# A two-stage expert kernel: the two choices of a token told apart by expert number, and the lower rows of five sequences gathered during the last choice tiles

## The chip, the cores and the metric

The kernel runs on one core of a Trainium2 chip. The metric is the time of one execution in device microseconds (us), the median of several runs. Engines work side by side: TensorE (PE, with its weight loads PEld), VectorE (DVE), ScalarE (ACT), GpSimd (POOL) and SyncE (SP), which here only issues DMAs. An engine takes its instructions in the order of its program and is held by waits on semaphores.

## The reference, cut to what matters

The input x has 16 sequences of 256 tokens with 256 features. A first block (attention, and eight experts with one choice for each token) adds to x. The second block is what the change touches. Every token chooses two of eight experts; a shared expert is added; the result goes, sequence by sequence, through two of eight gated experts.

```python
scores = softmax(logits)                     # a token's eight experts
topk_w, topk_idx = top_k(scores, 2)          # its two choices
topk_w = topk_w / (topk_w.sum(-1) + 1e-20)
y_all = einsum('etm,emh->eth', leaky(x @ w_gate) * (x @ w_up), w_down)
y = (y_all[topk_idx, token] * topk_w).sum(1) + p      # p: shared expert
...
logits = y.mean(axis=1) @ gate_w.T + gate_b  # per sequence
gates = softmax(two highest logits)
out = x + sum over the two e of gates[e] * gelu(y @ expert_w[e].T + expert_b[e])
```

The sum over a token's two choices has the same value in either order.

## The kernel before, in words

The choices of all tokens (2*4096) are sorted by expert into tiles of 128 rows; each expert begins a tile of its own, so there are TILES2 = 71 tiles at most. `pos_k_i[:, c, k]` is the place of choice k of the tokens of chunk c in the sorted order, `w_k` the choice's weight, `tstart2` the first tile of each expert.

The **choice stage** works tile by tile. POOL gathers the 128 input rows of a tile (`choice_rows`, an indirect DMA at L917, three buffers `c_gath`). TensorE transposes them (L1583), multiplies by the tile's expert (L1591), transposes the product three tiles later (`choice_turn`, L1599) and multiplies by the down weights (L1605). VectorE forms the product (L2860, L2862, tile i-1 in pass i of its loop) and copies the transposed product of tile i-3 out of PSUM (L2856); `choice_turn` of the next tile waits for that copy (`c_mtc`). ScalarE copies the result (`c_y`, three buffers), and SP stores it to `y2_dram` (L807), each store counted on one of three semaphores `c_st`.

The **gated stage** works on the 16 sequences b in order. When all stores of the choice stage have landed, POOL gathers for each sequence four times 128 rows of `y2_dram`: two chunks (n) of tokens by two choices (k). The buffers `yk` are three deep, so the gathers of sequence b wait for the sum of b-3 (`d_z`). Behind each gather is a memset on POOL (`space`, L947) on which POOL waits. VectorE's `sum_choices` (L2883, four instructions: k = 0 for both chunks, then k = 1) adds the weighted rows to the shared expert's result `p_s`. TensorE transposes the sum (`turn_z`, L1642), ScalarE copies it with its mean, TensorE multiplies for the gate logits (L1656), VectorE takes the two highest, and TensorE multiplies by the chosen experts (bias L1663, weights L1669). In one step TensorE does `turn_z(b)`, the rest of sequence b-1 and the first half expert of b; in the step of the last sequence one product of sequence 14 is ahead of `turn_z(15)`. VectorE's order in a step is: last addition of b-2, gates of b, first addition of b-1, sum of b+1. The first sums lie among the last shared experts.

At the start SP issues the loads of the first block; its last one is w1 (8 MB, L721). The next DMA in its queue is the store of the late rows `h_late` (L725), for which it waits on `hnorm`. This is the branch that the profiled run takes (`Else`).

Of the kernel before, what the change touches and what calls it, by code (L numbers as in the profile page):

```python
# [3 lines left out]
def bass_adaln_ffn_kernel(  # L4
# [18 lines left out]
    P = 128  # L23
# [31 lines left out]
    RT = 3  # L55
# [4 lines left out]
    with ctx:  # L60
# [300 lines left out]
        yk = [N.take(2 * NB, D) for _ in range(RT)]  # L361
        z_s = [N.take(NB, D) for _ in range(RT)]
        z_t = [N.take(KD, S) for _ in range(RT)]
# [44 lines left out]
        tile_f2 = Q.take(TILES2)  # L408

        NLB = NU // 4  # L410
        lgt_2 = Q.take(S)
        wt_g = router_g
# [122 lines left out]
        d_pos = sem("d_pos")  # L535
# [18 lines left out]
        d_got = [sem(f"d_got{k}") for k in range(3)]  # L554
# [13 lines left out]
        last_got = c_got[0:2]  # L568
        last_got0 = [16 * len(range(u, TILES2, RT)) for u in range(2)]
# [69 lines left out]
        def _(sp):  # L639
# [42 lines left out]

            general = branch(sp)

            with sp.If(general):
# [14 lines left out]

                sp.wait_ge(o_ps, B)
# [6 lines left out]
            with sp.Else():  # L708
# [12 lines left out]
                sp.dma_start(big_w[:, :], w1).then_inc(ld_w1, 16)  # L721

# [80 lines left out]
            for n in range(NEB):  # L803
                sp.dma_start(eb_rows[n:n + 1, :].rearrange("a (p k) -> a p k", k=EBW), eb_part[n]).then_inc(eb_set, 16)
            for i in range(TILES2):
                sp.wait_ge(c_yc, i + 1)
                sp.dma_start(y2_dram[i * P:(i + 1) * P, :], c_y[i % RT]).then_inc(c_st[i % RT], 16)  # L807
# [19 lines left out]
        def _(pool):  # L827
# [159 lines left out]

            for u in range(RT):
                pool.wait_ge(c_st[u], 16 * len(range(u, TILES2, RT)))

            def rows_again(b):
                hold(pool, d_e, 2 * B + E2 * b)
                pool.tensor_copy(pos_b[:, :, :], pos_k_i[:, bass.ds(b * NB, NB), :]).then_inc(d_pos, 1)
                hold(pool, d_pos, b + 1)
                for n in range(NB):
                    for k in range(2):
                        gather_rows(yk[0][:, 2 * n + k, :], y2_dram, pos_b[:, n, k:k + 1], d_back)

            for b in range(B):
                if b >= RT:  # L1000
                    pool.wait_ge(d_z, b - RT + 1)
                parts = ([(n, k, d_got[b % RT]) for n in range(NB) for k in range(2)] if b < B - 1 else
                         [(0, 0, last_got[0]), (1, 0, last_got[0]), (0, 1, last_got[1]), (1, 1, d_got[b % RT])])
                for n, k, done in parts:
                    gather_rows(yk[b % RT][:, 2 * n + k, :], y2_dram, pos_k_i[:, b * NB + n, k:k + 1], done)
                    space()
# [1844 lines left out]

# [218 lines left out]
```

## Time and profile before

| | us |
|---|---|
| median of 3 runs | 588.18 |
| lowest and highest | 587.75, 590.46 |
| the profiled execution | 589.62 |
| its span, first to last instruction | 587.9 |

| engine | busy us | share |
|---|---|---|
| PE | 558.1 | 95% |
| PEld | 463.4 | 79% |
| DVE | 321.1 | 55% |
| ACT | 243.1 | 41% |
| POOL | 233.9 | 40% |

The next four lines divide the span in 40 slices of 14.7 us. A digit is the busy share in tenths.

```profile
PE   7999999988999999999999989999999998998886
DVE  3877758676322225733538754444444344666665
POOL 2312211042111121007546365555555078777860
DMA  5960000186995522513395035565655322444441
```

The choice stage runs from about 340 to 468 us, the gated stage's gathers from 471 to 570 us. TensorE is busy in nearly all slices; its lowest shares are in the first slice and in the last four. POOL has a slice of 0 just ahead of the gated stage's gathers and then its highest shares. The DMA engines are idle in the slices from 44 to 103 us.

### The profile page before, as it was taken

How to read it: one execution, taken by the hardware profiler on the slowest of the kernel's cores; microseconds unless marked ns; L12 is line 12 of the kernel's file. 1: busy time of each engine (PE TensorE's matmuls, PEld its weight loads, DVE VectorE, ACT ScalarE, POOL GpSimd, SP SyncE). 2: the span in 40 equal slices, each digit the busy share in tenths (PEclk: the TensorE clock that was granted, in tenths of full speed). 3: DMA queues.
4: the chain of work that ended last, by engine and by line, in shares of the span. 5: the costliest groups of instructions: out<-in, count | busy, mean ns of one | idle time of the engine just before them, and what ended most of it. 6: DMA issues, size and time to landing. Idle time of an engine off the chain costs nothing.

```text
span 587.9 us, 11468 instructions
## 1 busy us (share of the span) xinstructions
PE 558.1 (95%) x3816; PEld 463.4 (79%) x3816; DVE 321.1 (55%) x967; ACT 243.1 (41%) x670; POOL 233.9 (40%) x319
## 2 busy tenths in 40 slices
PE   7999999988999999999999989999999998998886
PEld 4788887744999999988888968888878887776664
DVE  3877758676322225733538754444444344666665
ACT  1555444660211111116544245555555454443432
POOL 2312211042111121007546365555555078777860
PEclk9999999999999999999999999999999999999999
DMA  5960000186995522513395035565655322444441
GB/s 149 387 284 4 1 1 2 64 366 254 325 345 191 184 68 73 153 64 74 76 308 191 0 100 148 160 159 150 161 153 153 96 78 85 136 129 121 127 134 56
DMA packets 48853, 83.96 MB, mean 143 GB/s; under 512 B 8946, under 2 KB 41587, under 8 KB 47252
## 3 DMA queue, kind: packets, MB, share of 16 engines
q1 hardware_dynamic: 40676, 60.97, 29.7%
q0 software_dynamic: 8112, 22.16, 15.5%
q8 instruction: 36, 0.59, 0.4%
q14 instruction: 29, 0.24, 0.1%
HBM read 62.25 MB, written 20.84 MB: 141 GB/s over the span
## 4 chain that ended last, share of the span: by engine, by line
PE 70%; POOL 12%; DVE 5%; issue 5%; DMA 4%; ACT 2%; another core or an unknown queue 0%; SPq 0%; POOLq 0%; DVEq 0%; ACTq 0%
POOL arena L917 10%; PE psum L1331 10%; PE psum L1344 9%; PE psum L1591 9%; PE psum L1503 7%; PE psum L1605 5%; PE psum L1187 5%; PE psum L1159 5%; PE psum L1520 3%; PE psum L1583 3%; DMA arena<-x,row_tok 3%; POOL iota_i L947 2%; PE psum L1167 2%; PE psum L1538 1%; PE psum L1181 1%
## 5 line engine op out<-in xcount | busy, mean ns | idle before, releaser
L917 POOL DMA_INDIRECT arena<-x,row_tok x71 | 68.1, 959 | 55.7 <-PE psum L1583 47.2
L917 POOL DMA_INDIRECT arena<-y_sorted,pos_k_i x64 | 65.3, 1021 | 35.2 <-issue 16.1
L1591 PE MATMUL psum<-big_w,arena 128*128 x284 | 72.9, 379 | 0.0
L1927 ACT ACTIVATE arena<-psum,arena 128x128 f32<-128x128 f32 x64 | 18.2, 368 | 106.5 <-PE psum L1331 85.0
L1669 PE MATMUL psum<-big_w,arena 128*128 x248 | 61.3, 379 | 0.0
L1331 PEld LDWEIGHTS psum<-arena,big_w 128*128 128x128 f32 x512 | 59.5, 192 | 1.7 <-issue 1.0
L1331 PE MATMUL psum<-arena,big_w 128*128 128x128 f32 x512 | 59.8, 275 | 0.8 <-DVE arena L2624 0.8
L1503 PE MATMUL psum<-arena,big_w 128*128 128x256 f32 x256 | 59.9, 381 | 0.2 <-ACT arena L1946 0.2
L1591 PEld LDWEIGHTS psum<-big_w,arena 128*128 128x128 f32 x284 | 53.7, 190 | 7.2
L1344 PE MATMUL psum<-arena 128*128 128x256 f32 (+1 forms) x256 | 57.7, 379 | 0.0
L2860 DVE SCALAR_TENSOR_TENSOR arena<-arena 128x128 f32<-128x128 f32 x71 | 20.8, 293 | 62.2 <-ACT arena L2013 62.2
L1503 PEld LDWEIGHTS psum<-arena,big_w 128*128 128x128 f32 x256 | 47.3, 190 | 7.1 <-ACT arena L1946 0.9
L1344 PEld LDWEIGHTS psum<-arena 128*128 128x128 f32 x256 | 47.5, 190 | 5.8
L1669 PEld LDWEIGHTS psum<-big_w,arena 128*128 128x128 f32 x248 | 45.7, 190 | 6.7
L917 POOL DMA_INDIRECT arena<-h_late,row_tok x16 | 15.3, 959 | 81.7 <-PE psum L1319 69.6
L1605 PE MATMUL psum<-big_w,arena 128*128 x142 | 44.1, 392 | 1.3 <-ACT arena L2010 1.3
L892 POOL TENSOR_TENSOR arena<-arena 128x512 f32<-128x512 f32 x16 | 19.0, 1191 | 59.9 <-DVE arena L2223 59.8
L2010 ACT COPY arena<-psum 128x256 f32<-128x256 f32 x71 | 26.4, 372 | 22.2 <-PE psum L1605 19.5
L1187 PE MATMUL psum<-arena 128*128 128x256 f32 x144 | 32.7, 380 | 0.4 <-ACT arena L1806 0.4
L1159 PE MATMUL psum<-arena 128*128 128x128 f32 x256 | 32.6, 289 | 0.0
L1520 PE MATMUL psum<-big_w,arena 128*128 128x256 f32 x128 | 30.6, 382 | 1.3 <-ACT arena L1950 1.3
L1159 PEld LDWEIGHTS psum<-arena 128*128 128x128 f32 x256 | 31.4, 204 | 0.3 <-DVE arena L2223 0.2
(338 smaller groups left out, 997.8 us busy)
## 6 DMA issues: line engine op xcount, KB each, us to landing
y_sorted<-arena SPq DMA_DIRECT2D x71, 128.0 KB
big_w<-w SPq DMA_DIRECT2D x8, 1024.0 KB, 5.3
tokens<-x SPq DMA_DIRECT2D x4, 1024.0 KB, 13.3
x<-tokens SPq DMA_DIRECT2D x16, 256.0 KB, 2.6
out<-arena SPq DMA_DIRECT2D x15, 256.0 KB
y_late<-arena SPq DMA_DIRECT2D x16, 128.0 KB, 1.7
big_w<-expert_w_t SPq DMA_DIRECT2D x1, 2048.0 KB, 7.4
arena<-x,row_tok POOLq DMA_INDIRECT x71
```

What stands on the lines that cost most here:

```text
L917: pool.indirect_dma_start(dst, None, rows, bass.IndirectOffsetOnAxis(ap=idx, axis=0)).then_inc(done, 16)
L1159: mm = pe.matmul(bank[a][:, (j % 4) * P:(j % 4 + 1) * P], wq_s[:, k, j * P:(j + 1) * P], xt_l[:, k, :], start=k == 0, stop=k == KD - 1)
L1187: mm = pe.matmul(bank[6][:, 0:D], lhs(j), wo_s[:, j, :], start=j == 0, stop=j == NPAIR - 1)
L1331: mm = pe.matmul(bank[1 + 2 * u + f // 4][:, (f % 4) * P:(f % 4 + 1) * P], big_w[:, c:c + P], g_t[u][:, k, :], start=k == 0, stop=k == KD - 1)
L1344: mm = pe.matmul(bank[5 + j % 2][:, 0:D], act_t[j % 2][:, f, :], arena[:, bass.ds(e * (NF * D) + f * D, D)], start=f == 0, stop=f == NF - 1)
L1503: mm = pe.matmul(bank[up_bank(b) + q][:, half * S:(half + 1) * S], w[:, k, q * M1:(q + 1) * M1], p_s[:, unit(b)[1][k], :], start=k == 0, s ...
L1520: mm = pe.matmul(bank[6][:, n * D:(n + 1) * D], mid[u][q][:, n * P:(n + 1) * P], md_s[:, E1 + q, :], start=q == 0, stop=q == NSH - 1)
L1591: mm = pe.matmul(bank[2 + i % RT][:, 0:2 * M1], c_gt[i % RT][:, k, :], mgu_s[:, k, bass.ds(e, 1), :].rearrange("p a m -> p (a m)"), start= ...
L1605: pe.matmul(bank[5][:, 0:D], c_midt[i % RT], md_s[:, bass.ds(e, 1), :].rearrange("p a d -> p (a d)"), start=True, stop=True).then_inc(c_dn, 1)
L1669: mm = pe.matmul(o, z_t[u][:, k, n * P:(n + 1) * P], ew_s[:, k, bass.ds(e, 1), :].rearrange("p a d -> p (a d)"), start=False, stop=n == NB ...
L2010: act.copy(c_y[t % RT], bank[5][:, 0:D]).then_inc(c_yc, 1)
L2860: dve.scalar_tensor_tensor(c_mid[v], c_leak[v], 0.01, c_leak[v], ALU.mult, ALU.max).then_inc(c_lkd, 1)
```

## The change

The places of a token's two choices are put in order on VectorE: `pos_k_i[:, :, 0]` becomes the lower place (the expert with the lower number), `pos_k_i[:, :, 1]` the upper one, and the weights `w_k` are exchanged with them. Lower rows never lie in tiles of the last expert, so they are complete when the tiles ahead of `tstart2[7]` are stored; the number of stores on each `c_st` is worked out and read into registers on POOL. The lower rows get five buffers `y_lo` outside the memory of the choice stage, the upper ones three buffers `y_hi` in it. The lower rows of sequences 0 to 4 are gathered when POOL has issued its gathers of input rows and that number of stores is reached. Then, with all stores landed, come the upper rows of 0, 1 and 2, and from sequence 3 on: wait for the sum of b-3, upper rows of b, lower rows of b+2. So that no row of `y2_dram` is read that was never written, SP copies x over it early, in three DMAs from DRAM to DRAM (9088 rows of 1 KB), and waits for them ahead of the first store. TensorE's program is the same.

```diff
@@ memory @@
-        yk = [N.take(2 * NB, D) for _ in range(RT)]
+        y_hi = [N.take(NB, D) for _ in range(RT)]
         z_s = [N.take(NB, D) for _ in range(RT)]
+        assert N.at <= NC * D + RT * (2 * D + KD * P + 3 * M1)
+        N.at = NC * D + RT * (2 * D + KD * P + 3 * M1)
+        NLO = 5
+        y_lo = [N.take(NB, D) for _ in range(NLO)]
...
+        NFILL = -(-TILES2 * P // T)
@@ SP @@
+            def fill_choice():
+                for r0 in range(0, TILES2 * P, T):
+                    n = min(T, TILES2 * P - r0)
+                    sp.dma_start(y2_dram[r0:r0 + n, :], x[0:n, :]).then_inc(filled, 16)
...
                 sp.dma_start(wo_s, wo.rearrange("(j p) n -> p j n", p=P)).then_inc(ld_wo, 16)
                 sp.dma_start(big_w[:, :], w1).then_inc(ld_w1, 16)
+                fill_choice()
...
+            sp.wait_ge(filled, 16 * NFILL)
             for i in range(TILES2):
                 sp.wait_ge(c_yc, i + 1)
@@ POOL @@
             for i in range(TILES2):
                 choice_rows(i)
 
+            def low_rows(b):
+                for n in range(NB):
+                    gather_rows(y_lo[b % NLO][:, n, :], y2_dram, pos_k_i[:, b * NB + n, 0:1], d_lo[b % NLO])
+                    space()
+
+            def high_rows(b):
+                for n in range(NB):
+                    gather_rows(y_hi[b % RT][:, n, :], y2_dram, pos_k_i[:, b * NB + n, 1:2], d_hi[b % RT])
+                    space()
+
+            pool.wait_ge(table, 4)
+            for u in range(RT):
+                hold(pool, c_st[u], pool.value_load(stores_i[0:1, u:u + 1], min_val=16, max_val=16 * len(range(u, TILES2, RT))))
+            for b in range(NLO):
+                low_rows(b)
             for u in range(RT):
                 pool.wait_ge(c_st[u], 16 * len(range(u, TILES2, RT)))
+            for b in range(RT):
+                high_rows(b)
+            for b in range(RT, B):
+                pool.wait_ge(d_z, b - RT + 1)
+                high_rows(b)
+                if b + NLO - RT < B:
+                    low_rows(b + NLO - RT)
...
-            for b in range(B):
-                if b >= RT:
-                    pool.wait_ge(d_z, b - RT + 1)
-                parts = ([(n, k, d_got[b % RT]) for n in range(NB) for k in range(2)] if b < B - 1 else
-                         [(0, 0, last_got[0]), (1, 0, last_got[0]), (0, 1, last_got[1]), (1, 1, d_got[b % RT])])
-                for n, k, done in parts:
-                    gather_rows(yk[b % RT][:, 2 * n + k, :], y2_dram, pos_k_i[:, b * NB + n, k:k + 1], done)
-                    space()
@@ VectorE @@
+            def by_expert():
+
+                for u in range(RT):
+                    g = dve.tensor_scalar(first_i[:, u:u + 1], tstart2[:, E1 - 1:E1], float(RT - 1 - u), 21846.0, ALU.add, ALU.mult)
+                link(dve.tensor_tensor(lower, pos_k[:, :, 0], pos_k[:, :, 1], ALU.is_lt))
+                link(dve.tensor_scalar(first_i, first_i, 16, None, ALU.logical_shift_right))
+                dve.tensor_copy(first_f, first_i)
+                link(dve.tensor_scalar(higher, lower, -1.0, 1.0, ALU.mult, ALU.add))
+                dve.tensor_scalar(stores_i[:, :], first_f, 1.0, 16.0, ALU.max, ALU.mult)
+                dve.tensor_tensor(pos_k_i[:, :, 0], pos_k[:, :, 0], pos_k[:, :, 1], ALU.min)
+                link(dve.tensor_tensor(pos_k_i[:, :, 1], pos_k[:, :, 0], pos_k[:, :, 1], ALU.max))
+                dve.sem_inc(table, 1)
+                dve.tensor_tensor(w_lo, w_k[:, :, :], lower.unsqueeze(1).broadcast_to([P, 2, NC]), ALU.mult)
+                link(dve.tensor_tensor(w_hi, w_k[:, :, :], higher.unsqueeze(1).broadcast_to([P, 2, NC]), ALU.mult))
+                dve.tensor_tensor(w_k[:, 0, :], w_lo[:, 0, :], w_hi[:, 1, :], ALU.add)
+                dve.tensor_tensor(w_k[:, 1, :], w_lo[:, 1, :], w_hi[:, 0, :], ALU.add)
+
+            SORT_AT = 12
             for i in range(TILES2 + LAG):
                 if i >= LAG:
...
                     dve.tensor_tensor(c_mid[v], c_mid[v], bank[2 + v][:, M1:2 * M1], ALU.mult).then_inc(c_md, 1)
+                if i == SORT_AT:
+                    by_expert()
...
-                split = isinstance(b, int) and b == B - 1
-                if split:
-                    dve.wait_ge(last_got[0], last_got0[0] + 32)
-                else:
-                    hold(dve, d_got[u], 64 * turn_no + 64)
+                dve.wait_ge(d_lo[b % NLO], 32 * (b // NLO) + 32)
...
                 for k in range(2):
                     if k:
+                        dve.wait_ge(d_hi[u], d_hi0[u] + 32 * turn_no + 32)
                         hold(dve, d_z1, b + 1)
                     for n in range(NB):
-                        if split and k:
-                            dve.wait_ge((last_got[1], d_got[u])[n], (last_got0[1], 64 * turn_no)[n] + 16)
...
-                        m = dve.scalar_tensor_tensor(z_s[u][:, n, :], yk[u][:, 2 * n + k, :], w_k[:, k, bass.ds(b * NB + n, 1)], base,
+                        m = dve.scalar_tensor_tensor(z_s[u][:, n, :], (y_hi[u] if k else y_lo[b % NLO])[:, n, :], w_k[:, k, bass.ds(b * NB + n, 1)], base,
                                                      ALU.mult, ALU.add)
```

`link` adds a wait on VectorE's own semaphore behind an instruction.

## Rows read from the trace of the kernel before

**Rows 1.** Chain of waits of the last 148 us, shares by line

```profile
by line: POOL arena L917 40.3%; issue 15.7%; POOL iota_i L947 8.8%; PE psum L1591 6.4%; PE psum L1605 4.5%; PE psum L1669 4.2%; DMA arena<-x,row_tok 3.2%; DMA arena<-y_sorted,pos_k_i 1.8%; PE psum L1503 1.8%; PE psum L1583 1.7%; DMA y_sorte
```

**Rows 2.** Timeline (start us, us, engine line op tiles [idle before]), TensorE, turn_z

```profile
499.91 0.66 PE L1642 MATMUL psum<-ident,arena 128*128 128x128 f32 x4 [0.76 <-DVE arena L2883]
...
531.75 0.66 PE L1642 MATMUL psum<-ident,arena 128*128 128x128 f32 x4
...
568.37 0.66 PE L1642 MATMUL psum<-ident,arena 128*128 128x128 f32 x4 [0.64 <-DVE arena L2883]
...
575.01 0.60 PE L1642 MATMUL psum<-ident,arena 128*128 128x128 f32 x4
```

**Rows 3.** Timeline, VectorE, sums of sequences 0, 2 and 14

```profile
478.91 1.79 DVE L2883 SCALAR_TENSOR_TENSOR arena<-arena,w_k 128x256 f32<-128x256 f32 x4
...
498.06 1.79 DVE L2883 SCALAR_TENSOR_TENSOR arena<-arena,w_k 128x256 f32<-128x256 f32 x4
...
566.52 1.80 DVE L2883 SCALAR_TENSOR_TENSOR arena<-arena,w_k 128x256 f32<-128x256 f32 x4 [0.49 <-issue]
```

**Rows 4.** Timeline, POOL, gathers of input rows and of results

```profile
454.93 0.94 POOL L917 DMA_INDIRECT arena<-x,row_tok  x1 [0.73 <-PE psum L1583]
...
470.87 0.94 POOL L917 DMA_INDIRECT arena<-y_sorted,pos_k_i  x1 [15.00 <-DMA y_sorted<-arena]
...
472.31 0.95 POOL L917 DMA_INDIRECT arena<-y_sorted,pos_k_i  x1 [0.27 <-POOL iota_i L947]
...
501.17 0.95 POOL L917 DMA_INDIRECT arena<-y_sorted,pos_k_i  x1 [0.27 <-POOL iota_i L947]
...
533.80 0.95 POOL L917 DMA_INDIRECT arena<-y_sorted,pos_k_i  x1 [0.27 <-issue]
...
541.18 0.95 POOL L917 DMA_INDIRECT arena<-y_sorted,pos_k_i  x1 [0.27 <-issue]
...
563.37 0.95 POOL L917 DMA_INDIRECT arena<-y_sorted,pos_k_i  x1 [0.27 <-issue]
```

**Rows 5.** Busy time by stretch (PE, PEld, DVE, ACT, POOL, clock, DMA share, GB/s)

```profile
350.00:400.00 50.00, 48.29 (x261) 40.75 (x259) 22.73 (x88) 28.56 (x89) 27.72 (x30) 1.00 0.57 153
```

**Rows 6.** Timeline, VectorE, small instructions of both routings

```profile
136.59 0.17 DVE L2577 TENSOR_TENSOR arena<-arena 128x8 f32<-128x8 f32 x1
136.67 0.16 DVE L2578 TENSOR_TENSOR arena<-arena 128x8 f32<-128x8 f32 x1
136.87 0.17 DVE L2579 SCALAR_TENSOR_TENSOR arena<-arena 128x8 f32<-128x8 f32 x1
...
315.53 0.65 DVE L2805 TENSOR_SCALAR arena<-pos_k_i 128x64 int32<-128x64 int32 x1
...
316.21 0.20 DVE L2806 CAST arena<-arena 128x64 f16<-128x64 int32 x1
```

**Rows 7.** Timeline, copy and next transpose's weight load at the change's tile

```profile
364.03 0.28 DVE L2856 COPY arena<-psum 128x128 f32<-128x128 f32 x1
...
364.75 0.14 PEld L1599 LDWEIGHTS psum<-ident,arena 128*128 128x128 f32 x1
```

**Rows 8.** Timeline, TensorE, gate logits of 14 and last bias product

```profile
570.45 0.61 PE L1656 MATMUL psum<-big_w,arena 128*128 128x8 f32 x4 [0.55 <-ACT arena L2019]
...
578.58 0.39 PE L1663 MATMUL psum<-big_w,ones_bf 128*128 x1 [0.46 <-issue]
```

**Rows 9.** Timeline, SP's issues of w1 and of h_late

```profile
13.59 1.44 SPq L721 DMA_DIRECT2D big_w<-w  x1
...
111.23 0.29 SPq L725 DMA_DIRECT2D h_late<-arena  x1
```

**Rows 10.** DMA issues, 0 to 150 us: w1 (count, us from issue to landing)

```profile
big_w<-w SPq DMA_DIRECT2D x1, 28.0
```

**Rows 11.** Busy time by stretch, columns as in rows 5

```profile
10.00:20.00 10.00, 9.13 (x109) 8.52 (x108) 5.00 (x10) 2.84 (x6) 4.67 (x10) 1.00 0.96 217
...
40.00:50.00 10.00, 10.00 (x133) 8.55 (x131) 8.15 (x15) 5.74 (x12) 2.39 (x2) 1.00 0.01 2
```

More of the change, by code:

```diff
@@ L408, in bass_adaln_ffn_kernel @@
         tile_f2 = Q.take(TILES2)
+        first_i = Q.take(RT).bitcast(I32)
+        first_f = Q.take(RT)
+        stores_i = sb("stores_i", [P, RT], I32)
+        lower = Q.take(NC)
+        higher = Q.take(NC)
+        w_lo = Q.take(2, NC)
+        w_hi = Q.take(2, NC)
         NLB = NU // 4
         lgt_2 = Q.take(S)
+        assert N.at <= E0 * NF * D + Q.at
         wt_g = router_g
@@ L534, in bass_adaln_ffn_kernel @@
         d_back = sem("d_back")
-        d_pos = sem("d_pos")
         d_log = sem("d_log")
@@ L553, in bass_adaln_ffn_kernel @@
         c_st = [sem(f"c_st{k}") for k in range(3)]
-        d_got = [sem(f"d_got{k}") for k in range(3)]
+        d_lo = [sem(f"d_lo{k}") for k in range(NLO)]
+        filled = sem("filled")
         d_st = [sem(f"d_st{k}") for k in range(3)]
@@ L567, in bass_adaln_ffn_kernel @@
         half_st0 = 16 * len(range(0, TILES2, RT))
-        last_got = c_got[0:2]
-        last_got0 = [16 * len(range(u, TILES2, RT)) for u in range(2)]
+        d_hi, d_hi0 = c_got, [16 * len(range(u, TILES2, RT)) for u in range(RT)]
+        NFILL = -(-TILES2 * P // T)
         l_rows_ev, l_beat_g, ld_rest = ld_x[2], ld_x[1], ld_x[3]
@@ L721, in _ @@
                 sp.dma_start(big_w[:, :], w1).then_inc(ld_w1, 16)
+                fill_choice()
                 late_rows = h_late[1:, :].rearrange("(c p) d -> p c d", p=P)
@@ L986, in _ @@
                 choice_rows(i)
+            def low_rows(b):
[11 more added lines that the diff above has]
+                low_rows(b)
             for u in range(RT):
                 pool.wait_ge(c_st[u], 16 * len(range(u, TILES2, RT)))
+            for b in range(RT):
[5 more added lines that the diff above has]
+                    low_rows(b + NLO - RT)
             def rows_again(b):
                 hold(pool, d_e, 2 * B + E2 * b)
-                pool.tensor_copy(pos_b[:, :, :], pos_k_i[:, bass.ds(b * NB, NB), :]).then_inc(d_pos, 1)
-                hold(pool, d_pos, b + 1)
+                pool.tensor_copy(pos_b[:, :, :], pos_k_i[:, bass.ds(b * NB, NB), :]).then_inc(paced, 1)
+                hold(pool, paced, spaced[0] + b + 1)
                 for n in range(NB):
-                    for k in range(2):
-                        gather_rows(yk[0][:, 2 * n + k, :], y2_dram, pos_b[:, n, k:k + 1], d_back)
-            for b in range(B):
-                if b >= RT:
-                    pool.wait_ge(d_z, b - RT + 1)
-                parts = ([(n, k, d_got[b % RT]) for n in range(NB) for k in range(2)] if b < B - 1 else
-                         [(0, 0, last_got[0]), (1, 0, last_got[0]), (0, 1, last_got[1]), (1, 1, d_got[b % RT])])
-                for n, k, done in parts:
-                    gather_rows(yk[b % RT][:, 2 * n + k, :], y2_dram, pos_k_i[:, b * NB + n, k:k + 1], done)
-                    space()
+                    gather_rows(y_lo[0][:, n, :], y2_dram, pos_b[:, n, 0:1], d_back)
+                    gather_rows(y_hi[0][:, n, :], y2_dram, pos_b[:, n, 1:2], d_back)
             with pool.If(more_gates(pool)):
@@ L2992, in every_expert @@
                         base = z_s[0][:, n, :] if k else p_s[:, bass.ds(b * NB + n, 1), :].rearrange("p a d -> p (a d)")
-                        m = dve.scalar_tensor_tensor(z_s[0][:, n, :], yk[0][:, 2 * n + k, :], w_k[:, k, bass.ds(b * NB + n, 1)], base,
+                        m = dve.scalar_tensor_tensor(z_s[0][:, n, :], (y_hi if k else y_lo)[0][:, n, :], w_k[:, k, bass.ds(b * NB + n, 1)], base,
                                                      ALU.mult, ALU.add)
```

## The prediction, made before the changed kernel was run

> **What bounds the kernel now.** The change touches only the work from the choice tiles to the end, and I read that part from its end backwards. In the chain of waits over the last 148 us [rows 1], 40.3% is the GpSimd gather line L917 and 8.8% the memset L947 that spaces the gathers, against 4.2% for the gated experts' matmuls L1669. That share is no measure of the gain: it is counted along the one chain that ended last, and other limits stand close behind. The starts of a sequence's transposes (turn_z, L1642) show where gathers decide [rows 2]. From sequence 2 at 499.91 to sequence 8 at 531.75 a step takes 31.84/6 = 5.31 us, and sequence 8 starts with no idle time on PE. The next six steps, to sequence 14 at 568.37, take 36.62 us, 6.1 each, and at the end of them PE idles 0.64 us on VectorE's weighted sum L2883. That sum itself had to wait [rows 3]: sequence 14's starts at 566.52, after 0.49 us idle, and its last gather [rows 4] starts at 563.37, so it takes 0.95 to run and 2.2 more to land. Gathers thus bound only sequences 9 to 14. Before these the loop of transposes, copy, gate logits, gates on VectorE and next sum does, at 5.31 us.
>
> POOL stood idle 15.00 us before the first of these gathers [rows 4]: its last gather of input rows starts at 454.93, and then it waits for the last store of the choice tiles. In the stage of those tiles TensorE has no slack: 48.29 of 50 us busy [rows 5].
>
> **What the change does, part by part.** *The sort block at tile 12 costs time.* It puts 14 VectorE instructions (by_expert) behind product 11 and ahead of the copy L2856 that TensorE's next transpose needs. Five are followed by a wait on VectorE's own semaphore, nine are not. Small ones of this kind [rows 6] start 0.20 us after a waited one (136.87 after 136.67) and 0.08 after another (136.67 after 136.59): 5*0.20+9*0.08 = 1.7 us at 8 columns. Six here have 32 columns and two 64, where a cast lasts 0.20 instead of 0.17, so I take 2.0. A 64-column shift of integers lasts 0.65 [rows 6]; two or three at that price make 3.0, the upper bound. At that tile [rows 7] the copy runs from 364.03 to 364.31, and the weight load of the transpose that needs it starts at 364.75: a cover of 0.44. Nothing gives the rest back later, since TensorE is busy through every tile. Stall: 2.0-0.44 = **1.6 us lost**, between 1.3 and 2.6, and all that follows moves by it.
>
> *Ten gathers move into the idle 15 us.* The lower rows of sequences 0 to 4 need only tiles of experts 0 to 6. By the reference's routing of the drawn inputs expert 7 begins at tile 58 of 71, so the stores waited for come some ten tiles before the last, and have landed when POOL has issued its last input gather (454.93+0.94+1.6 = 457.5). Three register loads come first. No row shows one on POOL; the nearest is TensorE before a product that needs loaded numbers, 0.46 us idle for two [rows 8]. I take 1.1 for the three with their waits, bounds 0.5 and 3. Ten gathers at the pitch of 1.44 (472.31 after 470.87 [rows 4]) then end at 458.6+14.4 = 473.0, after the last store has landed (470.2+1.6 = 471.8). The two upper rows of sequence 0 have landed 2.9+2.2 us later, at 478.1; the sum takes them in its second half, at 478.91+1.6+0.9 = 481.4 [rows 3]. This first sum was not late before either, so the move gains nothing here; only the lead may count later. Beside the last tiles one gather per 1.44 us takes the place of one per tile (1.6 us), nearly the same load on the DMA engines, and I cost it at nothing, 0 to 0.5.
>
> *What the gain can be.* With no gather late, the six steps after 531.75 take 31.8 us instead of 36.6: 4.8. The step from 14 to 15 (6.64 us [rows 2]) has an order of its own; in it PE idles 0.55 us for ScalarE's copy, at the gate logits [rows 8], which may go too or come back. After 575.01 nothing waits for a gather. So 4.8 to 5.3 us, middle **5.05**.
>
> *What POOL gives back.* Ten gathers of lead are not kept. The upper rows of sequence b wait for sum b-3, and queued behind that wait are the lower rows of b+2, which sum b+2 needs. The early sums come when TensorE's order lets them, not when gathers land: sum 2 ends at 498.06+1.79+1.6 = 501.45 [rows 3], and only there may the upper rows of sequence 5 start. In the kernel before sequence 5 starts at 501.17 [rows 4]. Counted from there, the last upper row of 14 is gather 38 (the lower rows of 15 lie ahead of it), where it was gather 40: two fewer, not ten. It is also needed 0.9 us later, in the sum's second half. By the old stream it starts at 563.37-3.0+0.3 = 560.7 and lands at 563.8. It is needed at 564.2: turn of 14 at 531.75+31.8+1.6 = 565.2, less 1.9 from the sum's start to the turn (568.37-566.52), plus 0.9. In time by 0.4. But the old stream was quick in its second part, where VectorE was held back: 15 pitches of 1.48 from 541.18 to 563.37, against 20 of 1.63 from 501.17 to 533.80 at full pace; the four between took 7.4, 0.9 more than at 1.63 [rows 4]. All at 1.63, and with those 0.9 again, gather 38 starts at 501.45+37*1.63+0.9 = 562.7, lands at 565.8, **1.6 late**. Between 0 and 1.6 I take **0.8**, since a stream that is late slows VectorE and so comes back toward 1.48. Sequence 15's upper rows follow 2.9 us later before a step of 6.1: not late.
>
> The GPSIMD Engine Reference of the Trainium skill (Specifications) says that GpSimd shares its SBUF interface with VectorE and contends with its two-port modes and its instructions with two SBUF inputs. The sums have two such inputs, and the pitches of 1.63 and 1.48 agree with it. By that rule a VectorE that waits less makes the gathers slower, which is rival B below.
>
> *The copy of x into the sorted rows.* SP gets three more DMAs, 9.3 MB from DRAM to DRAM, queued behind w1 and ahead of the h_late stores [rows 9]. w1 is issued at 13.59 and lands 28.0 us later [rows 10], the stores come at 111.23, and from 40 us on the DMA engines are idle (share 0.01 [rows 11]). That leaves 111.2-41.6 = 69.6 us, so the copy is hidden from 134 GB/s up. No row shows a transfer from DRAM to DRAM; the nearest low rate of a busy stretch is 217 GB/s (10 to 20 us [rows 11]), at which it takes 43 us. Cost: nothing, and no gain, as nothing waits for it. The wait on "filled", ahead of the first store of choice rows after 345 us, is long satisfied.
>
> DMA: Bandwidth & Descriptors of the Trainium skill (Where 436 GB/s comes from) gives about 358 GB/s of HBM for a core. By that the copy takes 52 us, an estimate that counts its reads and its writes, and the sum stays the same.
>
> *Edits with one answer.* A sum has one more wait, satisfied while it waits for its own first half; the last sequence's split waits go; TensorE's order stays.
>
> **The sum.** On the profiled execution (589.62 us, of which 587.9 is the span; 1.4 above the median of 588.18): +1.6-5.05+0.8 = -2.65. On the median: **585.5 us**.
>
> **The rivals.** *A, the gathers are never late again.* For it: gather 38 in time by 0.4 at the old pitches. Against it: the pitch of 1.63. It gives 588.2+1.6-5.3 = 584.5, and 584.2 with the smallest stall.
> *B, gathers bound again, at 1.63.* For it: VectorE runs at full pace nearly all the way. It gives 588.2+1.6-5.05+1.6 = 586.4, and 587.7 with the dear sort block and the small gain.
> *C, the early gathers aren't early,* because POOL's register loads and waits take as long as the last stores. For it only that no row shows such a wait on POOL. All 64 gathers then follow the last store: 588.2+1.6 = 589.8, within what is called no change.
> *D, slower: the copy of x is still running when h_late must be stored.* It decides below 134 GB/s. At 100 it ends at 41.6+93 = 134.6 and moves all that follows by 23 us: 611. Against it: the rate of 217, and 70 us of gap.
>
> **How the numbers follow.** Chances: my forecast 0.35 (its own range 584.8 to 586.4), A 0.30, B 0.17, C 0.07, D 0.06, others 0.05. The bounds of the terms reach from 588.2+1.3-5.3 = 584.2 to 588.2+2.6-4.8+1.6 = 587.6; with the scatter of a median of such runs I give 583.8 to 587.9, which leaves out C and D. A measurement of this kernel can tell about 0.5%, 2.9 us, so faster means below 585.24. That is A and a third of my forecast, 0.42; the rest of it with B and C is 0.50; slower is D and a part of the others, 0.08.
>
> **What the profile after would show.** Right: 14 small VectorE instructions near 364 that take 2.0 us, and TensorE idle 1.6 us behind them; ten gathers from about 458.6 to 473; POOL idle before sequences 4 and 5; the turn of sequence 8 near 533.3, steps of 5.3 behind it, at most one or two of 12 to 14 with idle time under 1 us; the turn of 15 near 572.2. Wrong: a stall at tile 12 outside 1.3 to 2.6; POOL's pitch above 1.63; gaps in the steps of 9 to 12, which would make it B; the early gathers behind the last store, C; any new wait near 111 us, D, which would sink the whole sum.

## The result, and the profile after

The changed kernel takes 592.5 us (median of 14 runs, 590.3 to 597.0) beside 587.9 for the kernel before on the same chips (14 runs): the ratio is 1.0095, with a 95% interval of 1.0074 to 1.0116. It is slower by 5.6 us by the ratio, which compares runs on the same chip, and by 4.6 us by the two medians; 585.5 was predicted. Its profiled execution has a span of 591.0 us, against 587.9, so only 3.1 us of the loss can be read in the two traces.

Three marks of the timeline split that difference. The first h_late store (SP) tells how late everything is by then, the first turn_z when the last stage begins, the last turn_z how long its 15 steps took.

| mark | before | after | difference |
|---|---|---|---|
| first h_late store | 111.23 | 118.26 | +7.03 |
| from there to turn_z of sequence 0 (483.73, 491.63) | 372.50 | 373.37 | +0.87 |
| from there to turn_z of sequence 15 (575.01, 578.40) | 91.28 | 86.77 | -4.51 |
| from there to the end | 12.89 | 12.60 | -0.29 |

So the last stage gained what the change was expected to gain, and 7 us were lost ahead of 118 us, where the only new work is the copy of x. Timeline of the kernel after, TensorE alone (start us, us, engine line op tiles, count, and in brackets the idle time before and what ended it):

```profile
50.79 1.04 PE L1207 MATMUL psum<-ident,arena 128*128 128x128 f32 x8
56.63 1.15 PE L1200 MATMUL psum<-arena 64*64 64x65 f32 x32 [4.80 <-issue]
57.71 0.69 PE L1175 MATMUL psum<-ident,arena 128*128 128x128 f32 x2
58.32 1.15 PE L1200 MATMUL psum<-arena 64*64 64x65 f32 x32
```

The same place in the kernel before (its lines are 33 lower):

```profile
51.31 1.04 PE L1174 MATMUL psum<-ident,arena 128*128 128x128 f32 x8
53.08 0.69 PE L1167 MATMUL psum<-arena 64*64 64x65 f32 x32 [0.73 <-issue]
```

TensorE stands still for 4.80 us, and "issue" says that it waits for nothing that the profile shows: no tile, no semaphore. Nor is it one of the other engines; they wait for TensorE in that time. Ahead of the same instruction the kernel before has an idle 0.73 us of the same kind, which I had not read. At 65.82 us stands a second, shorter stop of the same kind:

```profile
65.82 1.50 PE L1192 MATMUL psum<-arena 128*128 128x128 f32 x12 [0.75 <-issue]
```

The stop is followed by a lower clock. Busy time by stretch (from:to, length, busy us and instructions of PE, PEld, DVE, ACT and POOL, TensorE's granted clock, DMA share, GB/s), after:

```profile
50.00:55.00 5.00, 1.83 (x13) 1.43 (x11) 0.00 (x0) 1.45 (x3) 0.00 (x0) 1.00 1.11 383
55.00:60.00 5.00, 3.37 (x70) 2.44 (x74) 2.10 (x4) 0.62 (x2) 0.00 (x0) 0.55 0.88 275
60.00:65.00 5.00, 5.00 (x36) 3.88 (x29) 4.11 (x8) 3.05 (x6) 2.38 (x2) 0.77 0.98 336
65.00:70.00 5.00, 4.25 (x27) 3.84 (x26) 1.76 (x5) 0.85 (x2) 0.00 (x0) 1.00 0.12 38
55.60:62.20 6.60, 5.57 (x79) 3.54 (x80) 4.10 (x6) 2.23 (x5) 1.19 (x1) 0.50 0.96 308
```

and before:

```profile
50.00:55.00 5.00, 4.26 (x85) 3.35 (x87) 1.19 (x3) 2.07 (x5) 0.00 (x0) 1.00 0.02 7
55.00:60.00 5.00, 5.00 (x47) 4.44 (x40) 4.83 (x9) 3.07 (x6) 2.38 (x2) 1.00 0.01 3
```

The DMA engines are full where they were empty. The 0.55 and the 0.77 are means over slices of two levels: from 55.60 to 62.20 us the granted clock is 0.50, the lower level of 1.2 GHz, and ahead of it and behind it 1.00. It fell when TensorE had been standing still since 51.83. Of the 7.03 us, 4.07 are the longer stop (4.80-0.73) and 0.75 the second one. The work between the stop and the next such cell (56.63 to 70.61 us without the second stop, 53.08 to 63.59 before) takes 2.7 us longer, in which the clock is low at first: the 32 small matmuls above take 1.15 instead of 0.69. The kernel after had been 0.5 us ahead when it came to the stop. At 70.61 the 7.0 us are complete.

The late stage, where it was predicted (turn_z, VectorE's block at tile 12, POOL's first gathers of results):

```profile
523.95 0.66 PE L1675 MATMUL psum<-ident,arena 128*128 128x128 f32 x4
...
566.88 0.66 PE L1675 MATMUL psum<-ident,arena 128*128 128x128 f32 x4
```

```profile
370.13 0.27 DVE L2888 TENSOR_SCALAR arena<-arena 128x1 int32<-128x1 f32 x3
...
372.21 0.28 DVE L2907 COPY arena<-psum 128x128 f32<-128x128 f32 x1
...
372.64 0.30 PE L1632 MATMUL psum<-ident,arena 128*128 128x128 f32 x1 [1.38 <-DVE arena L2907]
```

```profile
462.64 0.95 POOL L937 DMA_INDIRECT arena<-x,row_tok  x1 [0.67 <-PE psum L1616]
465.33 0.95 POOL L937 DMA_INDIRECT arena<-y_sorted,pos_k_i  x1 [1.73 <-DMA y_sorted<-arena]
466.76 0.95 POOL L937 DMA_INDIRECT arena<-y_sorted,pos_k_i  x1 [0.27 <-issue]
```

The turns of sequences 5 and 13 lie 42.93 us apart with no idle time before any between them: 5.37 a step, also from sequence 8 on, where [rows 2] has 6.1. The sort block takes 2.08 us and stops TensorE for 1.38. POOL's 15.00 idle us of [rows 4] are 1.73. Of the +0.87 between h_late and the first turn the stall of 1.38 is a part; the rest of that stretch came out 0.5 shorter. In the seven profiles whose kernel has the sort block in one piece this stretch lies between 371.28 and 373.99 us, a spread that no experiment here explains.

### The profile page after: what moved, and what is told of

The parts are those of the page before. It is cut to its first block, busy times and chain, and to the rows that moved or that the text cites. A ratio compares the mean times of both kernels' runs of the same rounds, so it can differ in the third digit from the quotient of the medians.

```text
span 591.0 us, 11515 instructions
## 1 busy us (share of the span) xinstructions
PE 560.7 (95%) x3816; PEld 464.7 (79%) x3816; DVE 321.4 (54%) x981; ACT 243.4 (41%) x670; POOL 232.2 (39%) x319
## 4 chain that ended last, share of the span: by engine, by line
PE 79%; DVE 8%; issue 5%; ACT 3%; DMA 3%; POOL 1%; SPq 0%; DVEq 0%; ACTq 0%
PE psum L1364 10%; PE psum L1377 9%; PE psum L1536 9%; PE psum L1624 9%; PE psum L1638 5%; PE psum L1220 5%; PE psum L1702 5%; PE psum L1192 5%; PE psum L1553 4%; PE psum L1616 3%; DMA arena<-x,row_tok 2%; PE psum L1200 2%; PE psum L1571 1%; PE psum L1214 1%; PE psum L1689 1%
## 5 line engine op out<-in xcount | busy, mean ns | idle before, releaser
L937 POOL DMA_INDIRECT arena<-y_sorted,pos_k_i x64 | 63.9, 999 | 30.0 <-issue 16.6
L2911 DVE SCALAR_TENSOR_TENSOR arena<-arena 128x128 f32<-128x128 f32 x71 | 20.8, 292 | 61.2 <-ACT arena L2046 55.5
L1220 PE MATMUL psum<-arena 128*128 128x256 f32 x144 | 32.7, 380 | 0.4 <-ACT arena L1839 0.4
L2046 ACT COPY arena<-psum 128x128 f32<-128x128 f32 x71 | 18.8, 265 | 32.0 <-issue 24.5
```

Source lines behind the costliest of these rows:

```text
L937: pool.indirect_dma_start(dst, None, rows, bass.IndirectOffsetOnAxis(ap=idx, axis=0)).then_inc(done, 16)
L1220: mm = pe.matmul(bank[6][:, 0:D], lhs(j), wo_s[:, j, :], start=j == 0, stop=j == NPAIR - 1)
L2911: dve.scalar_tensor_tensor(c_mid[v], c_leak[v], 0.01, c_leak[v], ALU.mult, ALU.max).then_inc(c_lkd, 1)
```

## The experiments

All ratios are to the kernel before on the same chip; "stop" is TensorE's idle time of kind issue ahead of the small matmuls (the first late scores of a cell).

**First question: is it the copy, and is it its packets?** The copy of x adds 9.3 MB in only 144 packets of 56 or 64 KB (with some of 4 bytes 192 in all, 48 KB on average). My first theory (F) was that a fetch of instructions has to wait behind such packets.

Before, plus the copy alone:

```diff
                 sp.dma_start(big_w[:, :], w1).then_inc(ld_w1, 16)
+                fill_choice()
...
+            sp.wait_ge(filled, 16 * NFILL)
```

> The kernel before with one thing added: the copy of x into the sorted rows (three transfers from DRAM to DRAM, 9.3 MB, issued behind w1) and its wait ahead of the first choice store. No sort by expert, no early gathers. Theory F: the copy alone costs what the trace of the changed kernel lost early: TensorE stops for about 5 us near 52 us while it waits for nothing that the profile shows (the engines fetch their instructions over the same DMA engines, behind packets of some 48 KB), and its clock then falls. So all work from 111 us on is 6 to 8 us late: about 595, ratio 1.010 to 1.014. Rival S: the early loss has another cause (another order of the program, other code addresses) and the copy is hidden as predicted: within 0.5 us of before.

Measured: 598.8 us, 1.0151 [1.0119, 1.0183]; the first h_late store at 118.10. Its stop:

```profile
56.53 1.14 PE L1178 MATMUL psum<-arena 64*64 64x65 f32 x32 [5.51 <-issue]
```

The copy alone brings the early loss whole, 6.9 us, with a second stop too (1.36 us at 65.67). Rival S falls. The other 3 us of its profile lie in the last stage (94.2 us from first to last turn instead of 91.3), where ScalarE waits up to 3.62 us for something that the profile puts outside this core's engines; the copy has long landed by then, and this is not explained.

The changed kernel without the copy:

```diff
                 sp.dma_start(big_w[:, :], w1).then_inc(ld_w1, 16)
-                fill_choice()
...
-            sp.wait_ge(filled, 16 * NFILL)
...
+                rows = y2_dram[0:58 * P, :] if b < NLO else y2_dram
```

> The changed kernel without the copy of x. So that nothing unwritten is read, the lower gathers of sequences 0 to 4 name only the first 58 of the 71 tiles of sorted rows, which hold all rows that they need for the drawn inputs; their number, size and time are the same. Theory F: the early 7 us come back and the rest of the change stays (the sort block +1.4 to +2, steps 9 to 15 -4.5, the end -0.3): 588 - 3 = 585, ratio 0.993 to 0.997. Rival S: no better than the changed kernel, 592 to 593.

Measured: 589.3 us, 0.9996 [0.9964, 1.0028]. The early loss is gone (stop 0.92, h_late at 110.46), but the ratio is not the 0.995 that I expected. In its profile two late steps take 6.05 and 6.75 us, in which TensorE's gate logits wait up to 1.46 us for ScalarE's copy, with all gathers landed. No other profile with early gathers has late steps of that length for that reason. Its stretch from h_late to the first turn, 373.99 us, is long as well. Beside the kernel below that holds the copy back (371.28 and 86.77) the two stretches are 2.7 and 2.4 us longer. So this run alone does not show that the copy costs the whole loss; it shows that the early stop goes with the copy. The rest stays open.

The same bytes in rows of 1 KB:

```diff
-                    sp.dma_start(y2_dram[r0:r0 + n, :], x[0:n, :]).then_inc(filled, 16)
...
+                        sp.dma_start(to[t, r0:r0 + n, :], of[t, 0:n, :]).then_inc(filled, 16)
```

> The changed kernel with the same 9.3 MB copied in rows of 1 KB (even rows and odd rows, six transfers), so that no packet is longer than 1 KB; issued at the same place. Theory F in its form with packet size (a fetch of instructions waits behind a few packets of 48 KB): the stop near 52 us is gone or under 1 us and the time is that of the kernel without the copy, about 585 (0.993 to 0.997). Rival M (memory or the share of the DMA engines is what counts, whatever the packets): the copy takes as long or longer, TensorE stops again for 3 us or more, and the time stays at 591 to 594.

Measured: 591.5 us, 1.0041 [1.0014, 1.0068]; h_late at 116.99.

```profile
55.98 1.15 PE L1203 MATMUL psum<-arena 64*64 64x65 f32 x32 [4.23 <-issue]
```

12500 packets between 10 and 110 us instead of 3600, and the stop is 4.23 instead of 4.80. The length of a packet is not the cause; this part of F falls.

The copy ahead of w1:

```diff
+                fill_choice()
                 sp.dma_start(big_w[:, :], w1).then_inc(ld_w1, 16)
-                fill_choice()
```

> The changed kernel with the copy issued ahead of w1 instead of behind it. The same packets, earlier. Theory F: the stop stands wherever an instruction fetch meets the copy, so it moves to before 50 us or to more than one place, and w1 lands later, near 60 us, which only the expert part at 111 us and on needs. Loss again 3 to 9 us: 589 to 595. Rival T (the loss is one fetch that happens to fall near 52 us, and none falls where the copy now runs): the loss is gone, 585.

Measured: 591.2 us, 1.0032 [1.0002, 1.0061]; a stop of 4.93 ahead of the same instruction (56.07), none elsewhere. The copy's last transfer is issued by 16.7 us and lands 32.7 us later, before the stop begins at 51.13, and w1 lands only 53.0 us after its issue. So what fills the DMA engines during this stop is w1, a load, and no longer the copy. Neither F (the stop moves) nor T (it vanishes) had it so: it stands at one place of the program, whatever is being transferred there.

**Second question: what is at that place?** TensorE's program has two cases, and the late one is cut in two, with the other case between the parts (lines of the kernel before):

```python
            NEAR = 3
            with pe.If(late):            # L1377
                for c in range(NEAR):
                    attend_late(c)
            with pe.Else():
                ...
            with pe.If(late):            # L1427
                for c in range(NEAR, NTW):
                    attend_late(c)
```

Behind the third cell TensorE jumps over the whole other case, and the stop stands ahead of the first instruction of the fourth. The list of DMA queues for 50 to 58 us names what a jump has to fetch (packets, MB, share of 16 engines), before:

```profile
q8 instruction: 3, 0.05, 2.3%
```

and after:

```profile
q1 hardware_dynamic: 61, 2.95, 110.2%
q8 instruction: 1, 0.02, 0.9%
```

Instructions come over the same DMA engines in packets of 16 KB. Theory J: TensorE can go on after the jump only when those at its target have come, and beside a full load of data that takes 4 to 5 us instead of 0.7. The Trainium skill (Runtime: NRT & Kernel Launch, section Instruction fetch mechanics) states the first half: a taken branch whose target isn't already buffered forces a DMA fetch before execution goes on. The traces agree with it in all twelve profiles. The last 16 KB packet of q8 ahead of the late scores lands 1.7 to 2.0 us before these start, whatever the length of the stop. Eight of the twelve (all in us; those of kernels told further below stand here too, to be read together):

| kernel | TensorE stops | packet starts | packet has landed | TensorE goes on |
|---|---|---|---|---|
| before | 52.35 | 50.43 | 51.36 | 53.08 |
| changed, no copy | 51.39 | 49.46 | 50.59 | 52.31 |
| changed, copy held back | 51.86 | 49.94 | 50.98 | 52.71 |
| changed | 51.83 | 53.76 | 54.89 | 56.63 |
| before, copy alone | 51.03 | 53.67 | 54.81 | 56.53 |
| rows of 1 KB | 51.75 | 52.94 | 54.03 | 55.98 |
| copy ahead of w1 | 51.13 | 53.34 | 54.28 | 56.07 |
| before, jump at cell 1 | 28.03 | 32.35 | 33.36 | 35.20 |

With idle DMA engines the packet starts 1.8 to 1.9 us before TensorE has run out of work; under load it starts 1.2 to 4.3 us after. Once it has started it takes no longer than otherwise (0.94 to 1.13 us under load, 0.93 to 1.41 without). So the time is lost before the packet starts, not in its transfer.

The changed kernel with the jump two cells later:

```diff
-            NEAR = 3
+            NEAR = 5
```

> The changed kernel with one number changed, NEAR = 3 to 5: TensorE's program for the late attention is cut into two branches, cells 0 to NEAR-1 and the rest, and between them lies the program for the other case, over which TensorE has to jump. Both branches' work and its order are the same; only the jump moves, from some 52 us (while the copy of x runs, until 67) to some 75 us. Theory J (the stop is the jump: the instructions behind it have to be fetched by DMA, and that fetch stands behind the copy's packets): no stop near 52, one of 0.7 to 1.2 us near 75, clock at 1.00 from 50 on, the h_late store near 112; time as without the copy, ratio 0.996 to 1.002. Rival F (any instruction fetch under the copy stops TensorE, the jump has no part in it): a stop of 3 us or more still stands before 67 us and the time stays at 1.006 or more.

Measured: 584.9 us, 0.9957 [0.9934, 0.9979], a little below the 0.996 to 1.002 expected; h_late at 110.87.

```profile
50.75 1.04 PE L1207 MATMUL psum<-ident,arena 128*128 128x128 f32 x8
51.72 0.69 PE L1200 MATMUL psum<-arena 64*64 64x65 f32 x32
```

```profile
73.69 1.04 PE L1207 MATMUL psum<-ident,arena 128*128 128x128 f32 x8
75.67 0.70 PE L1200 MATMUL psum<-arena 64*64 64x65 f32 x32 [0.93 <-issue]
```

The copy is where it was (it lands 52.6 us after its issue), and yet the fourth cell starts without a stop. From 50 to 60 us TensorE is busy throughout, at full clock, beside a full DMA load:

```profile
50.00:60.00 10.00, 10.00 (x133) 8.50 (x132) 7.24 (x13) 5.74 (x12) 2.38 (x2) 1.00 1.03 336
```

So it is the jump that meets the load, not the copy as such. An ordinary fetch under this load (a 16 KB packet from 56.60 to 57.77) costs nothing here. That isn't so in every run: the second stops of the changed kernel (0.75) and of the copy alone (1.36) stand in straight code, in the middle of a group of matmuls, and end 1.50 and 1.32 us after a 16 KB packet that landed at 64.32 and 64.35. In both the stop at the jump came first.

The kernel before, no copy, with the jump two cells earlier, so that it meets w1:

```diff
-            NEAR = 3
+            NEAR = 1
```

> The kernel before, without any copy, with NEAR = 3 changed to 1, so that the same jump falls near 30 us, while w1 is on its way (DMA share over 1 from 20 to 30 us). Theory J: TensorE stops there for 3 to 5 us where it stopped 0.73 us near 53 us before, and its clock may fall behind it; the h_late store is 2.5 to 6 us later, ratio 1.004 to 1.010. Rival M (only a copy from DRAM to DRAM does it, a load such as w1 does not): a stop under 1.2 us and the ratio within 0.003 of 1.

Measured: 593.5 us, 1.0122 [1.007, 1.0174]; h_late at 117.90.

```profile
26.93 1.09 PE L1174 MATMUL psum<-ident,arena 128*128 128x128 f32 x8 [0.54 <-DVE arena L2231]
35.20 1.15 PE L1167 MATMUL psum<-arena 64*64 64x65 f32 x32 [7.17 <-issue]
```

```profile
28.00:35.20 7.20, 0.03 (x2) 0.04 (x1) 0.00 (x0) 0.70 (x2) 0.00 (x0) 0.78 0.99 422
```

A load into SBUF does it too, here with 7.17 us, beyond the 3 to 5 expected, with the clock at 0.66 in the stretch from 30 to 40 us; time and h_late (6.7 us later) also lie beyond what was expected. Rival M falls. Why it is longer here isn't shown. The rate of the transfers doesn't order the stops: during this one DMA moved 422 GB/s, from 52 to 56 us it moved 315 in the changed kernel (stop 4.80) and 463 with the copy ahead of w1 (stop 4.93).

The changed kernel with the copy held back until the jump is done:

```diff
                 sp.dma_start(big_w[:, :], w1).then_inc(ld_w1, 16)
+                sp.wait_ge(late_qk, 2 * 3 + 1)
                 fill_choice()
```

> The changed kernel with the copy of x held back until TensorE is past the jump (SyncE waits for the first scores of cell 3, near 53 us, ahead of the three transfers). The copy then runs from about 53 to 80 us or somewhat longer. Theory J: TensorE's stop at 52 is back at 0.7 to 1.2 us, at most one more of under 1 us while the copy runs, h_late near 111 to 112, ratio 0.996 to 1.002. Rival F: the stop moves with the copy, 3 us or more between 55 and 85 us, ratio 1.006 or more.

Measured: 584.4 us, 0.9941 [0.9919, 0.9964], better than the 0.996 to 1.002 expected; h_late at 110.87. The jump at 52.71 costs 0.85, and the copy then runs beside a TensorE that is never idle (sum over 53 to 80 us):

```profile
53.00:80.00 27.00, 27.00 (x362) 22.60 (x354) 19.86 (x36) 13.49 (x29) 5.92 (x5) 1.00 0.95 319
```

One wait on SyncE turns the slower kernel into a faster one. Over the profiles the jump costs 0.73, 0.75, 0.85, 0.92, 0.93, 0.95 and 1.21 us with idle DMA engines, and 4.23, 4.80, 4.93, 5.51 and 7.17 with busy ones.

**Third question: what are the parts of the late stage worth?** All three kernels hold the copy back, so the one just told (581.8 us of span, turns at 482.15 to 568.92) is their measure.

No early gathers: all 64 follow the last store, and the three register loads on POOL go.

```diff
             for u in range(RT):
-                hold(pool, c_st[u], pool.value_load(stores_i[0:1, u:u + 1], min_val=16, max_val=16 * len(range(u, TILES2, RT))))
-            for b in range(NLO):
-                low_rows(b)
-            for u in range(RT):
                 pool.wait_ge(c_st[u], 16 * len(range(u, TILES2, RT)))
             for b in range(RT):
+                low_rows(b)
                 high_rows(b)
+            for b in range(RT, NLO):
+                low_rows(b)
```

> The changed kernel with the copy of x held back behind the jump, but without the early gathers: all 64 gathers of the last stage start when the last store of the choice tiles has landed, in the order lower and upper rows of sequence 0, 1 and 2, then lower rows of 3 and 4; from there on as in the changed kernel. Nothing is left out. Theory (the gain of the change is the lead of ten gathers and nothing else): the gathers bind again from about sequence 8 on, steps of 5.7 to 6.3 us as in the kernel before, first to last turn 90 to 92 us instead of 86.8, and the whole change is then its stall at tile 12 and nothing more: ratio 0.999 to 1.005. Rival (the order by halves alone, with sums that take their upper rows late, brings most of it): first to last turn 87 to 89 us, ratio 0.995 to 0.998.

Measured: 590.7 us, 1.0056 [1.003, 1.0082]. First POOL, then turn_z:

```profile
469.56 0.95 POOL L938 DMA_INDIRECT arena<-y_sorted,pos_k_i  x1 [15.16 <-DMA y_sorted<-arena]
```

```profile
525.16 0.66 PE L1675 MATMUL psum<-ident,arena 128*128 128x128 f32 x4
530.91 0.66 PE L1675 MATMUL psum<-ident,arena 128*128 128x128 f32 x4 [0.52 <-DVE arena L2931]
537.81 0.65 PE L1675 MATMUL psum<-ident,arena 128*128 128x128 f32 x4 [1.66 <-DVE arena L2931]
544.20 0.66 PE L1675 MATMUL psum<-ident,arena 128*128 128x128 f32 x4 [1.16 <-DVE arena L2931]
```

POOL's 15 idle us are back, the gathers bind from sequence 8 on, and first to last turn takes 93.4 us instead of 86.8. The lead of ten gathers is worth those 6.7 us. The rest of the change costs more than its stall at tile 12: 93.4 is beyond the 90 to 92 expected and 2.1 us above the kernel before, and the ratio is just above its range. What those 2.1 us are was not tested.

The sort block spread over tiles 12 to 16, and the wait for the upper rows ahead of the sum:

```diff
+                if i >= SORT_AT:
+                    next(sort_parts, None)
...
                 dve.wait_ge(d_lo[b % NLO], 32 * (b // NLO) + 32)
+                dve.wait_ge(d_hi[u], d_hi0[u] + 32 * turn_no + 32)
...
-                        dve.wait_ge(d_hi[u], d_hi0[u] + 32 * turn_no + 32)
```

> As the kernel with the copy held back behind the jump, and two things more: the 14 instructions of the sort by expert are spread in five parts over the tiles 12 to 16, behind the copy for TensorE's next transpose and ahead of the next product (expected: no stall of 1.4 us at tile 12, 0 to 0.4 in all), and in each sum the wait for the upper rows stands ahead of the sum's first instruction instead of in its middle (expected: a sum takes 1.80 us instead of 1.86 and a step 5.31 instead of 5.365 as long as no gather is late, 0.8 us in all over 15 steps; where the upper rows land within the sum's first half the step gets later instead, by up to 0.9 us). Theory: 2 us less than the kernel with the copy held back, ratio to before 0.991 to 0.998. Rival: the late steps are bound by the gathers again because the wait comes 0.9 us earlier, and it gives the 0.8 back: 0.996 to 1.001.

Measured: 584.7 us, 0.9957 [0.9933, 0.9981]. Sums on VectorE:

```profile
548.64 1.79 DVE L2938 SCALAR_TENSOR_TENSOR arena<-arena,w_k 128x256 f32<-128x256 f32 x4
554.56 1.80 DVE L2938 SCALAR_TENSOR_TENSOR arena<-arena,w_k 128x256 f32<-128x256 f32 x4 [0.55 <-DMA arena<-y_sorted,pos_k_i]
560.93 1.80 DVE L2938 SCALAR_TENSOR_TENSOR arena<-arena,w_k 128x256 f32<-128x256 f32 x4 [0.99 <-DMA arena<-y_sorted,pos_k_i]
```

A sum takes 1.79 again and most steps 5.30, but two of the last three wait for their gathers (5.92 and 6.37 us). POOL's last gather starts 78.5 us after the first turn (559.90) where it was 78.7 (560.88): faster sums bring no faster gathers. The 0.8 won is given back and as much again: first to last turn takes 87.55 us beside 86.77. The ratio lies at the edge between the two ranges and decides nothing; by the rows, the rival was right about the gathers.

The spread alone, with the wait left in the middle of the sum:

```diff
+                if i >= SORT_AT:
+                    next(sort_parts, None)
...
-                if i == SORT_AT:
-                    by_expert()
```

> The changed kernel with the copy of x held back behind the jump and the sort by expert spread over tiles 12 to 16; the wait for the upper rows stays in the middle of each sum. Theory: no stall of 1.37 us at tile 12 (0 to 0.4 in all); steps of 5.36 us with no gather late, since the sums leave the gathers 0.06 us more a step and 0.9 us more in each sum: first to last turn 86.8 us, as with the copy held back alone, so 1 to 1.5 us below that kernel, ratio 0.990 to 0.995. Rival: the run with the wait at the front was as good, both at 0.994 to 0.997.

Measured: 583.3 us, 0.9937 [0.9913, 0.9962], span 581.6. No stall at tile 12, and steps of 5.37 with no gather late (86.77 from first to last turn). The gain over the kernel that holds the copy back is too small for these intervals (0.9941). In its profile TensorE has a stall of 1.31 at 350.62, behind ScalarE, where the other has 1.01 behind a gather: this stage varies by as much between executions as the sort block costs. It has the lowest median of all, 3.7 us below the kernel before.

## Why the prediction was wrong, step by step

**The copy of x, "Cost: nothing": the step that failed.** I asked only whether it ends before the h_late stores. That part was right: it landed near 68 us, 43 us before 111, and rival D did not occur. (Alone on the DMA engines, in the run that holds it back, its last transfer landed 30.1 us after its issue, where the two rates of the prediction gave 43 and 52.) But I took as hidden what no later transfer waits for, and did not ask what else uses the DMA engines between 40 and 68 us, since [rows 11] show them idle. TensorE's own instructions use them, at a jump that lay in the code I had and showed as 0.73 idle us at 53.08 in the trace I had. The term is +7.0 us, by a path that the prediction did not have: the fetch behind the jump comes late, TensorE stands still, and its clock is at the lower level for a while. Taking it away by moving either side of the meeting leaves 584.9 and 584.4.

**The sort block: right.** 2.0 us predicted, 2.08 measured; a stall of 1.6 predicted, 1.38 measured.

**Ten gathers into the idle 15 us: right.** Predicted to start 3.7 us after the last input gather, measured 2.7, at the pitch of 1.44.

**The gain of 5.05: right mechanism, with one term left out.** Steps fell to the loop's own pace and the step from 14 to 15 from 6.64 to 6.15. But that pace is 5.37 and not 5.31. I costed the second wait of a sum at nothing, as it is satisfied by then; the sum took 1.86 instead of 1.79. Over 14 steps that is 0.8 us, and 5.05-0.8 = 4.25 stands beside 4.51 measured.

**POOL gives back 0.8: wrong, it was 0.** No gather was late, as in rival A. I had read that POOL is quick (1.48) only where VectorE is held back, and costed the late case with 1.63 throughout. In the changed kernel VectorE is never held back there, and yet the 20 gathers from 508.54 to 541.36 have a pitch of 1.64 and the 19 to 570.36 one of 1.53. So the slow first half has another cause, which the runs don't show, and these pitches don't speak for gathers that slow down when VectorE waits less. Gather 38 starts 59.4 us behind the end of sum 2 (507.79 to 567.15), beside 59.2 by the old stream and 61.2 with 1.63: the first of my two estimates was the right one. How little was to spare, the run with the wait at the front shows: there two sums waited 0.55 and 0.99. That run has both faster steps and upper rows needed 0.9 us earlier in a sum; which of the two made them late is not separated.

**The sum.** With the terms as measured and the copy at nothing: +1.4-4.5 = -3.1, so 585.1; the kernels whose copy does not meet the jump took 584.9 and 584.4, and rival A had 584.5. With the copy at +7.0 instead, the sum is +3.9, or 592.1, beside the 592.5 measured. The late stage was read well enough. My range had no case for a cost of the copy other than at h_late, and the one thing that I named to look for it, a wait near 111 us, was the wrong place.

One slip in the rivals: D's 611 leaves out the gain of the late stage, with which it is 609.

**Left open.** Why the kernel without the copy measured 0.9996 and not 0.995, with two long late steps behind ScalarE's copy; the extra 3 us of the last stage in the kernel with the copy alone; the 2.1 us that the change without its lead costs in the last stage; and why one stop was 7.17 us. The packets' times show that a fetch under load is late in starting and not slow in its transfer. What holds it up ahead of its start, the runs do not tell; they show only that size and order of the packets matter little.

## What to carry to other kernels

A transfer that nothing waits for is not free until you know what shares the DMA engines with it: list the long jumps of an engine's program and keep bulk transfers away from them, or put the jump where DMA is idle. (Only a branch of TensorE was measured here; other engines and the ends of loops were not.) In a profile, look for idle time ended by "issue" ahead of the first instruction behind a branch; it is small when DMA is idle, and a copy placed beside it makes it several times as long. And a lead is used up by a user that is faster than its supplier: POOL needs some 6.3 us for the four gathers of a sequence (61.8 us for 39 of them), and TensorE's step takes 5.37. Cost what speeds up the user together with what supplies it.

## What the runs showed of the hardware

- A jump of TensorE over a long piece of program cost 0.73 to 1.21 us with idle DMA engines, 4.23 to 5.51 beside a copy from DRAM to DRAM at some 300 to 315 GB/s (52 to 56 us), and 4.93 and 7.17 beside a load into SBUF at 463 and 422 GB/s.
- In all twelve profiles TensorE went on 1.7 to 2.0 us after a 16 KB instruction packet had landed. Under load this packet started 1.2 to 4.3 us after TensorE had stopped, without load 1.8 to 1.9 us before; its own time was 0.9 to 1.4 us in both cases.
- Straight code under the same load (1.03 of the engines' share, 50 to 60 us) cost TensorE nothing where no stop at a jump came first; behind such a stop it cost 0.75 and 1.36 us in two profiles, and nothing in two others.
- After a stop of 4.8 us the granted clock was 0.50, the lower level of 1.2 GHz, from 55.60 to 62.20 us; where the stop was 0.73, it stayed at 1.00 from 50 to 60 us.
- A copy of 9.3 MB from DRAM to DRAM ran at about 320 GB/s alone (53 to 80 us), counted as the DMA list counts it, each byte once.
- One more wait on a semaphore that is already at its value, in the middle of a sum of four VectorE instructions, made the sum 1.86 us instead of 1.79 and a step 5.37 instead of 5.30.
